# Four attention layers on a graph: where the rows of the node ranges and the first block's one-hot rows are made and loaded

## The chip, the cores and the metric

One core of a Trainium2 chip runs the kernel. The metric is the time of one execution on the device, in microseconds (us); the profile's span runs from the first to the last instruction of the profiled execution.

## The reference, cut to what matters

The model has 3125 nodes with 48 features and 100,000 edges (`src`, `dst`, sorted by `dst`). It runs four small graph networks one after the other. The change touches the first of them, a block of four attention layers (`L = 4`, `H = 48`, `RBF = 40`):

```python
for i in range(L):
    Q = _ln(h @ Wq[i], gq[i], bq[i])
    K = _ln(h @ Wk[i], gk[i], bk[i])
    qi = Q[src]
    kj = K[dst]
    score = (qi * kj).sum(-1) + 0.1 * (edge_attr * qi[:, :RBF]).sum(-1) + logm[dst]
    smax = jax.ops.segment_max(score, src, num_segments=N)
    es = jnp.exp(jnp.minimum(score - smax[src], 20.0))
    denom = jax.ops.segment_sum(es, src, num_segments=N)
    alpha = es / (denom[src] + 1e-10)
    m = h[dst] @ Wm[i]
    aggi = jax.ops.segment_sum(alpha[:, None] * m, src, num_segments=N)
    z = jnp.concatenate([h, aggi], axis=-1) @ Wu[i]
    z = jnp.where(z > 0, z, 0.01 * z)
    h = _ln(h + z, go[i], bo[i])
```

## The kernel before, in words

**Nodes and edges.** The nodes stand in 25 blocks of 128 (`NB = 25`, `P = 128`). The edges were sorted earlier into 25 blocks by `src`, and within each block into 38 tiles (`KT`) of 128 edges. 37 of these tiles (`NW`) belong to node ranges of `dst`: range `k` is the 128 nodes from `WIN[k]` on. The first 24 ranges (`FINE`) overlap and start at `round(1536 * (k / 24) ** 2)`; the other 13 are the node blocks 12 to 24 themselves. The 38th tile holds edges that fit in no range.

**A layer** is one turn of a hardware loop (`nc.Fori(0, LAYERS)` in `first_part`) over four stages: `node_rows`, `attend`, `cold_softmax`, `node_update`. A stage is a block with one instruction stream for each engine; it ends when all five engines have reached its end, and a barrier of all engines follows (`stage`, line 86 in the profile's rows).

**`node_rows`** makes the rows of all nodes. It goes through five chunks `i` of five node blocks (`CS`): ScalarE and VectorE normalise the products, then split each row into three bf16 parts: ScalarE the upper two (`upper`), VectorE the last (`parts`). The parts of the keys and values go to the SBUF tile `tabp`, those of the queries to `queryp`. SyncE (SP) waits for a chunk's parts and writes `table` (line 908) and `queries` (line 909) to HBM. TensorE makes one last small product at the stage's end (line 955) and waits for ScalarE's copy `wmT` for it.

**`attend`** works on units `u`, four (`q` = 0 to 3, the tile ranges `TAKE[q]`) for each edge block `i`. For a unit, `keys` lets TensorE pick the rows of the edges' ends by one-hot products (line 1578 from the SBUF tile `near`, which holds the rows of the 37 ranges; line 1580 from `queryp`); ScalarE copies (1672); GpSimd (POOL) adds the edge attributes (1536, `add_attr`); VectorE multiplies and sums (1709, 1712). `keys` of unit `u` waits for ScalarE's copy of unit `u - 1` and for VectorE's product of unit `u - 2`:

```python
if u:
    pe.wait_ge(s_rowk, u)
if u >= 2:
    pe.wait_ge(s_dot, u - 1)
```

`add_attr` of the first unit of a block also waits for that block's load of `attr`. SP issues all loads, in the order of its program: ten rows of ranges (`rows_of_nodes(0)`, line 1492), the two one-hot tiles of block 0 (`first(0)`, lines 1498 and 1499), the other 27 ranges, and then `attributes(0)` (line 1504) and what the next blocks need. TensorE starts the stage with `READY = 36` products of 512 columns whose result nobody reads (line 1637).

Of the kernel before, what the change touches and what calls it, by code (L numbers as in the profile page):

```python
# [18 lines left out]
P = 128  # L19
# [9 lines left out]
FINE = 24  # L29
# [831 lines left out]

def node_rows(nc, c, ps, a, layer, h, logm, vec, wqk, wm, wmT, wub, wu, queryp, table, queries, acc, nmax, m):

# [8 lines left out]
    needs = [(s.stop - 1) // 4 + 1 for s in CS]  # L872
    W = H1 + KH
    hT = m.sb("nr_hT", [H, NP])
    qk = m.sb("nr_qk", [P, NB, 2, H])
# [13 lines left out]
    with stage(nc, "node_rows", "w", "vec", "wu", "link", "centred", "scaled", "cols", "turned", "hT", "qk", "got", "sq", "var",  # L889
               "std", "both", "rest", "parts", "upper", "wm", "wmT", "wmu", "wu2", "out") as (  # L890
            block, s_w, s_vec, s_wu, s_link, s_centred, s_scaled, s_cols, s_turned, s_hT, s_qk, s_got, s_sq, s_var, s_std,
            s_both, s_rest, s_parts, s_upper, s_wm, s_wmT, s_wmu, s_wu2, s_out):
        @block.sync
        def _(sp):
            sp.dma_start(wqk[:, 0:H], at(a["Wq"])).then_inc(s_w, 16)
            sp.dma_start(wqk[:, H:2 * H], at(a["Wk"])).then_inc(s_w, 16)
            for n, v in enumerate(["gq", "bq", "gk", "bk"]):
                sp.dma_start(vec[:, n, :], row(a[v])).then_inc(s_vec, 16)
            sp.dma_start(wm[:], at(a["Wm"])).then_inc(s_wu, 16)
            sp.dma_start(wub[:], a["Wu"][bass.ds(layer, 1), H:2 * H, :].rearrange("o k f -> (o k) f")).then_inc(s_wu, 16)  # L900
            sp.dma_start(wu[0:H, :], a["Wu"][bass.ds(layer, 1), 0:H, :].rearrange("o k f -> (o k) f")).then_inc(s_wu, 16)
            for n, v in enumerate(["go", "bo"]):
                sp.dma_start(vec[:, 4 + n, :], row(a[v])).then_inc(s_wu, 16)
            for i, s in enumerate(CS):
                rows = lambda t: t.rearrange("(b p) w -> p b w", p=P)[:, s, :]
                sp.wait_ge(s_parts, 2 * (i + 1))
                sp.wait_ge(s_upper, 4 * (i + 1))
# [3 lines left out]
            sp.wait_ge(s_out, 32 * NC)  # L911

# [10 lines left out]
        def _(pe):  # L923
# [30 lines left out]
            pe.wait_ge(s_wmT, 1)  # L954
            pe.matmul(ps[64:64 + H, 6, 0:H], wmT[:], wub[:], start=True, stop=True).then_inc(s_wmu, 1)

        @block.scalar
        def _(act):
# [17 lines left out]
            def upper(i):  # L976
                s, x, r = CS[i], high(both[:, CS[i], :]), high(rest[:, i % 2])
                act.wait_ge(s_both, i + 1)
                act.copy(queryp[:, s, 0, :], x[:, :, 0:H1]).then_inc(s_upper, 1)
                act.copy(tabp[:, s, 0, :], x[:, :, H1:W]).then_inc(s_upper, 1)  # L980
                act.wait_ge(s_rest, i + 1)
                act.copy(queryp[:, s, 1, :], r[:, :, 0:H1]).then_inc(s_upper, 1)
                act.copy(tabp[:, s, 1, :], r[:, :, H1:W]).then_inc(s_upper, 1)
            done = 0
# [17 lines left out]
        def _(dve):  # L1002
# [440 lines left out]

def attend(nc, c, ps, m, lists, table, near, queryp, dead, sel, off, acc, nmax, spill_dst):

# [13 lines left out]
    VB = 4  # L1459
    READY = 36  # L1460
# [3 lines left out]
    hotT_s, hotT_d = m.sb("at_hotT_s", [P, 4, KT, P], F8), m.sb("at_hotT_d", [P, 4, NW, P], F8)  # L1464
    key = m.sb("at_key", [P, 2, 10, H1])
# [11 lines left out]
    rings = [f"attr{k}" for k in range(2)] + [f"hots{k}" for k in range(2)] + [f"hotT{k}" for k in range(4)] + [  # L1477
        f"far{k}" for k in range(4)] + [f"near{k}" for k in range(Q)]
    turned_bank = ps[:, 7, 128:192].bitcast(BF16)
    with stage(nc, "attend", *names, *rings) as (  # L1480
            block, s_keys, s_rowk, s_key, s_dot, s_score, s_split, s_turned, s_rows, s_laid, s_top, s_max, s_mgot, s_shift,
            s_prob, s_h, s_val, s_rest, s_split2, s_sum, s_added, s_link, *dmas):
        s_attr, s_hots, s_hotT, s_far, s_near = dmas[0:2], dmas[2:4], dmas[4:8], dmas[8:12], dmas[12:]

        @block.sync
        def _(sp):
            flat = lambda v, k: v[:, k].rearrange("p k e -> p (k e)")

# [68 lines left out]
        def _(pe):  # L1557
# [5 lines left out]
            def keys(i, q):  # L1563
                u = Q * i + q
                if q == 0:
                    pe.wait_ge(s_hotT[i % 4], 32 * (i // 4 + 1))
# [58 lines left out]
            def total(i, q):  # L1625
# [846 lines left out]
def first_part(nc, c, m, ps, a, x, h, tmp, table0, embs, embp, mult, logm, list1, lists, spill_dst, starts, mask, trips, base, w1,  # L2472
# [45 lines left out]
    with nc.Fori(0, LAYERS) as layer:  # L2518
        with ExitStack() as ctx0:
            node_rows(nc, c, ps, a, layer, h, logm[:], vec, wqk, wm, wmT, wub, wu, queryp, table, queries, acc[:], nmax[:],  # L2520
                      Memory(nc, ctx0))
        with ExitStack() as ctx0:
            t = Memory(nc, ctx0)
            near = t.sb("near", [P, NW, 3, KH], BF16)
            attend(nc, c, ps, t, lists, table, near, queryp, dead, sel, off, acc, nmax, spill_dst)
        with ExitStack() as ctx0:
# [1066 lines left out]
```

## Time and profile before

| | us |
|---|---|
| median of three runs | 5786.9 |
| lowest and highest run | 5772.91 and 5797.48 |
| the profiled execution's own time | 5777.92 |
| its span, first to last instruction | 5776.3 |
| mean granted TensorE clock in it (1.0 is 2.4 GHz) | 0.816 |

All stages come one after the other on one core, so each microsecond that a stage boundary moves is one of the total, unless a later stage waits for something else. The first layer's `node_rows` starts at 1914 us of the span and its `attend` at 1956 us; the other three layers repeat the pattern. The rows of the next but one section are from the first layer where no more is said.

### The profile page before, as it was taken

The page shows a single profiled execution, that of the slowest core. Times are in us where ns is not written, and L with a number is a line of the kernel's source. Part 1 is how long each engine was busy: PE and PEld are TensorE (multiplying, and loading weights), DVE is VectorE, ACT ScalarE, POOL GpSimd, SP SyncE. Part 2 cuts the span into 40 slices and gives each one's busy share as a digit, 9 for nine tenths or more (in the row PEclk, how much of TensorE's full clock was granted, in tenths as well). Part 3 has the DMA queues.
Part 4 walks back from the last instruction along what each step waited for, and adds up shares of the span by engine and source line. Part 5 has one row for each costly group of instructions (what it writes and reads, how often), then busy time and mean ns, then how long its engine had stood idle before and what let it go on. Part 6 is the DMA issues. An engine that isn't in the chain of part 4 may idle for free. (4 is left out here: it accounts for less than half of the span.)

```text
span 5776.3 us, 186815 instructions
## 1 busy us (share of the span) xinstructions
PE 4309.7 (75%) x79576; PEld 3592.7 (62%) x79576; DVE 3791.9 (66%) x7925; ACT 2250.1 (39%) x7746; POOL 2681.4 (46%) x2702
## 2 busy tenths in 40 slices
PE   7999994046666499759976997599757845877887
PEld 4555552035555388748874887488735733877786
DVE  6888875079998588657765785687576446545244
ACT  3333331046666255435543554355401424101310
POOL 2777777756666177517751775277520510000000
PEclk7666665569998699869987998799877977988897
DMA  9322223167775344234423442344255434000000
GB/s 352 74 73 74 70 68 74 42 150 197 195 201 166 113 161 165 92 109 167 154 92 120 157 154 92 123 154 165 80 88 196 158 106 134 2 9 4 4 4 10
DMA packets 488184, 656.80 MB, mean 114 GB/s; under 512 B 316480, under 2 KB 370372, under 8 KB 484117
## 3 DMA queue, kind: packets, MB, share of 16 engines
q1 hardware_dynamic: 450965, 595.00, 32.7%
q0 software_dynamic: 33856, 48.44, 3.4%
q8 instruction: 645, 10.57, 0.7%
q14 instruction: 222, 1.82, 0.1%
q10 hardware_dynamic: 2496, 0.98, 0.1%
HBM read 464.16 MB, written 180.09 MB: 112 GB/s over the span
## 5 line engine op out<-in xcount | busy, mean ns | idle before, releaser
L299 POOL DMA_INDIRECT edges<-sb_bk_rec,sb_bk_pos x782 | 784.8, 1004 | 323.7 <-issue 234.0
L1688 ACT ACTIVATE sb_at_val<-banks,sb_at_prob 128x49 f32<-128x49 f32 x3800 | 776.0, 326 | 189.7 <-PE banks L1622 183.3
L1727 DVE TENSOR_REDUCE sb_at_tops<-banks 128x1 f32<-128x512 f32 x1000 | 652.5, 661 | 279.1 <-PE banks L1602 276.7
L1578 PE MATMUL banks<-sb_near,sb_at_hotT_d 128*128 128x49 bf16 x11100 | 610.3, 184 | 74.0 <-DVE sb_at_key L1709 44.5
L1536 POOL TENSOR_TENSOR sb_at_key<-sb_at_key,sb_at_attr 128x400 f32<-128x400 f32 (+1 forms) x400 | 371.8, 930 | 581.1 <-ACT sb_at_key L1672 489.9
L1580 PE MATMUL banks<-sb_queryp,sb_at_hotT_s 128*128 128x49 bf16 x11400 | 624.5, 185 | 12.8 <-issue 12.3
L1578 PEld LDWEIGHTS banks<-sb_near,sb_at_hotT_d 128*128 128x128 fp8e4 x11100 | 560.3, 96 | 79.1 <-issue 69.3
L1580 PEld LDWEIGHTS banks<-sb_queryp,sb_at_hotT_s 128*128 128x128 fp8e4 x11400 | 559.5, 96 | 15.7 <-issue 15.7
L1543 POOL TENSOR_TENSOR sb_at_val<-sb_at_val 128x490 f32<-128x490 f32 (+1 forms) x400 | 387.4, 968 | 68.9 <-ACT sb_at_val L1688 67.4
L1672 ACT COPY sb_at_key<-banks 128x490 f32<-128x490 f32 (+1 forms) x400 | 225.3, 563 | 462.9 <-PE banks L1580 460.6
L1545 POOL TENSOR_TENSOR sb_at_val<-sb_at_val 128x490 f32<-128x490 f32 (+1 forms) x400 | 386.6, 966 | 31.4
L1622 PE MATMUL banks<-sb_near,sb_at_hotT_d 128*128 128x49 bf16 x11100 | 358.5, 186 | 34.3 <-ACT sb_at_val L1688 22.6
L1602 PE MATMUL banks<-sb_at_rows,sb_sel 114*128 114x128 bf16 x3800 | 379.0, 220 | 1.2 <-issue 1.2
L1599 PE MATMUL banks<-sb_at_hotT_s,sb_off 128*128 128x512 fp8e4 x1000 | 369.4, 369 | 7.3 <-issue 4.5
L1602 PEld LDWEIGHTS banks<-sb_at_rows,sb_sel 114*128 114x128 bf16 x3800 | 297.0, 97 | 116.1 <-issue 9.2
L1622 PEld LDWEIGHTS banks<-sb_near,sb_at_hotT_d 128*128 128x128 fp8e4 x11100 | 331.7, 97 | 43.1 <-ACT sb_at_val L1688 29.1
L1633 PE MATMUL banks<-sb_at_val,sb_at_hot_s 128*128 128x147 bf16 x3800 | 342.3, 237 | 11.9 <-issue 9.1
L1709 DVE TENSOR_TENSOR sb_at_key<-banks,sb_at_key 128x490 f32<-128x490 f32 (+1 forms) x400 | 253.1, 633 | 143.5 <-POOL sb_at_key L1536 143.5
L1262 POOL TENSOR_TENSOR sb_gt_msg<-sb_gt_msg 128x245 f32<-128x245 f32 (+1 forms) x175 | 239.8, 1370 | 189.9 <-DVE sb_gt_msg L1409 189.2
L1633 PEld LDWEIGHTS banks<-sb_at_val,sb_at_hot_s 128*128 128x128 fp8e4 x3800 | 281.1, 101 | 14.4 <-issue 10.7
L2902 PE MATMUL banks<-sb_conv_parts,sb_C 128*128 128x144 bf16 x3750 | 249.3, 232 | 30.8 <-DVE sb_conv_parts L2852 30.8
L2902 PEld LDWEIGHTS banks<-sb_conv_parts,sb_C 128*128 128x128 bf16 x3750 | 247.6, 101 | 31.9 <-DVE sb_conv_parts L2852 31.9
(692 smaller groups left out, 10166.0 us busy)
## 6 DMA issues: line engine op xcount, KB each, us to landing
sb_at_attr<-attr SPq DMA_DIRECT2D x100, 760.0 KB, 7.5
sb_at_hotT_s<-rows_src_t SPq DMA_DIRECT2D x100, 608.0 KB, 3.9
sb_at_hot_s<-rows_src SPq DMA_DIRECT2D x100, 608.0 KB, 8.6
sb_at_hotT_d<-rows_dst_t SPq DMA_DIRECT2D x100, 592.0 KB, 5.9
edges<-sb_pad SPq DMA_DIRECT2D x95, 460.0 KB, 7.0
sb_gt_rec<-edges SPq DMA_DIRECT2D x25, 1748.0 KB
sb_we_hotT<-rows_dst_t SPq DMA_DIRECT2D x52, 592.0 KB, 5.8
attr<-sb_gt_rec SPq DMA_DIRECT2D x25, 760.0 KB, 13.2
```

Source lines behind the costliest of these rows:

```text
L299: pool.indirect_dma_start(list1, bass.IndirectOffsetOnAxis(pos[:, t:t + 1], 0), rec[:, k, j, :], None).then_inc(sent[k], 16)
L1536: pool.tensor_tensor(key[:, u % 2, 0:n, 0:RBF], key[:, u % 2, 0:n, 0:RBF], attr[:, i % 2, a:b, :], ALU.add).then_inc(s_key, 1)
L1543: pool.tensor_tensor(x[:, 0:n, 1, :], x[:, 0:n, 0, :], halves(0), ALU.subtract).then_inc(s_rest, 1)
L1545: pool.tensor_tensor(x[:, 0:n, 2, :], x[:, 0:n, 1, :], halves(1), ALU.subtract).then_inc(s_split2, 1)
L1578: pe.matmul(ps[:, 0, H1 * j:H1 * j + H1], where, what, start=(n == 0), stop=(n == 2))
L1580: ins = pe.matmul(ps[:, 1 + u % 2, H1 * j:H1 * j + H1], hotT_s[:, i % 4, k, :], queryp[:, i, n, :], start=(n == 0), stop=(n == 2))
L1602: ins = pe.matmul(bank[:, P * j:P * j + P], sel[:, k, :], rows[:, i % 2, :], start=False, stop=(k == ks[-1]))
L1622: ins = pe.matmul(ps[:, 5, H1 * j:H1 * j + H1], where, what, start=(n == 0), stop=(n == 2))
L1633: ins = pe.matmul(ps[:, 6, 0:3 * H1], hot_s[:, i % 2, k, :], high(val[:, v % VB, j].rearrange("p n f -> p (n f)")), start=(k == 0), stop=( ...
L1688: ins = act.mul(val[:, v % VB, j, 0, :], ps[:, 5, H1 * j:H1 * j + H1], prob[:, i % 2, k:k + 1])
L1727: dve.tensor_reduce(tops[:, i % 2, g:g + 1], ps[:, 3 + x % 2, 0:P * len(RG[g])], AX, ALU.max).then_inc(s_top, 1)
L2902: return pe.matmul(ps[:, d % AHEAD, 0:3 * H], C[:, s, P * d:P * d + P], rows(s), start=(s == 0), stop=(s == NB - 1))
```

## The change

Four things change in the layers' stages; what is computed stays the same.

1. `near` and the one-hot tiles are allocated outside both stages. VectorE and ScalarE write the parts of node blocks 12 to 24 straight into `near`, where ranges 24 to 36 stand (`homes`); SP writes `table` from there. Only blocks 0 to 11 stay in `tabp`. The chunk of blocks 10 to 14 falls in two pieces.
2. SP loads the 24 overlapping ranges from `table` within `node_rows` (`windows`, line 936), each group behind a wait for the landing of the table chunks that it reads.
3. SP loads the two one-hot tiles of block 0 within `node_rows` (`ahead`, line 920), ahead of the first table chunk.
4. The 36 products of TensorE move from the start of `attend` to the end of `node_rows` (line 996).

`attend` no longer has loads of `near`, nor the wait for them.

```diff
+    LOW = WIN[FINE] // P
+    READY = 36
+    FINE_OF = [[k for k in range(FINE) if all(WIN[k] + P <= P * s.stop for s in CS[i:i + 1]) and
+                (i == 0 or WIN[k] + P > P * CS[i - 1].stop)] for i in range(NC)]
-    tabp = m.sb("nr_tabp", [P, NB, 3, KH], BF16)
+    tabp = m.sb("nr_tabp", [P, LOW, 3, KH], BF16)
+    def homes(s):
+        low, top = range(s.start, min(s.stop, LOW)), range(max(s.start, LOW), s.stop)
+        kept = [(slice(low[0], low[-1] + 1), tabp[:, low[0]:low[-1] + 1])] if low else []
+        return kept + ([(slice(top[0], top[-1] + 1), near[:, FINE + top[0] - LOW:FINE + top[-1] + 1 - LOW])] if top else [])
...
-                sp.dma_start(rows(table), tabp[:, s].rearrange("p b i f -> p b (i f)")).then_inc(s_out, 16)
-                sp.dma_start(rows(queries), queryp[:, s].rearrange("p b i f -> p b (i f)")).then_inc(s_out, 16)
+            for to, src in ahead:
+                sp.dma_start(to, src).then_inc(s_ahead, 16)
+            def write(i):
+                s = CS[i]
+                sp.wait_ge(s_parts, sum(PARTS[:i + 1]))
+                sp.wait_ge(s_upper, sum(UPPER[:i + 1]))
+                for bs, to in homes(s):
+                    sp.dma_start(rows(table, bs), to.rearrange("p b i f -> p b (i f)")).then_inc(s_table[i], 16)
+                sp.dma_start(rows(queries, s), queryp[:, s].rearrange("p b i f -> p b (i f)")).then_inc(s_out, 16)
+            def windows(i):
+                for j in range(i + 1):
+                    sp.wait_ge(s_table[j], 16 * len(homes(CS[j])))
+                for k in FINE_OF[i]:
+                    sp.dma_start(near[:, k].rearrange("p i f -> p (i f)"), table[WIN[k]:WIN[k] + P, :]).then_inc(s_near, 16)
+            write(0)
+            write(1)
+            windows(0)
+            write(2)
+            windows(1)
+            write(3)
+            windows(2)
+            write(4)
             sp.wait_ge(s_wu, 80)
...
             pe.matmul(ps[64:64 + H, 6, 0:H], wmT[:], wub[:], start=True, stop=True).then_inc(s_wmu, 1)
+            for _ in range(READY):
+                pe.matmul(ps[:, 7, :], c["identb"][:], along(c["identb"][:], 4), start=True, stop=True)
...
-                dve.tensor_tensor(tabp[:, s, 2, :], r[:, :, H1:W], high(r)[:, :, H1:W], ALU.subtract).then_inc(s_parts, 1)
+                for bs, to in homes(s):
+                    of = slice(bs.start - s.start, bs.stop - s.start)
+                    dve.tensor_tensor(to[:, :, 2, :], r[:, of, H1:W], high(r)[:, of, H1:W], ALU.subtract).then_inc(s_parts, 1)
...
-            rows_of_nodes(0)
-            first(0)
-            for q in range(1, Q):
-                rows_of_nodes(q)
             attributes(0)
...
-                if i == 0:
-                    pe.wait_ge(s_near[q], 16 * sum(k < NW for k in TAKE[q]))
...
-            for _ in range(READY):
-                pe.matmul(ps[:, 0, :], c["identb"][:], along(c["identb"][:], 4), start=True, stop=True)
```

**SP's order, end of `node_rows` and start of `attend`.** `nr_tabp` is `tabp`, `rows_src_t` and `rows_dst_t` are the one-hot rows in HBM; `x10` counts equal issues. Before:

```order
L908 DMA table<-sb_nr_tabp 128x5x294
L909 DMA queries<-sb_queryp 128x5x147
L83 UNCONDITIONAL_BRANCH
L1485 UNCONDITIONAL_BRANCH
L1492 DMA sb_near<-table 128x294 x10
L1498 DMA sb_at_hotT_s<-rows_src_t 128x4864
L1499 DMA sb_at_hotT_d<-rows_dst_t 128x4736
L1492 DMA sb_near<-table 128x294 x27
L1504 DMA sb_at_attr<-attr 128x1520
```

The same stretch of SP's program in the changed kernel, from the second table chunk to the first load of `attend`:

```order
L928 DMA table<-sb_nr_tabp 128x5x294
L929 DMA queries<-sb_queryp 128x5x147
L936 DMA sb_near<-table 128x294 x14
L928 DMA table<-sb_nr_tabp 128x2x294
L928 DMA table<-sb_near 128x3x294
L929 DMA queries<-sb_queryp 128x5x147
L936 DMA sb_near<-table 128x294 x7
L928 DMA table<-sb_near 128x5x294
L929 DMA queries<-sb_queryp 128x5x147
L936 DMA sb_near<-table 128x294 x3
L928 DMA table<-sb_near 128x5x294
L929 DMA queries<-sb_queryp 128x5x147
```

37 loads of ranges and two of one-hot rows stood between the stage's branch and `attr`; now 24 loads stand between the table chunks of `node_rows`, and `attr` is the first issue of `attend`.

**TensorE's order at the boundary of the two stages.** Before, from the last product of `node_rows` (`sb_wub`, `sb_wmT`) on:

```order
L955 MATMUL banks<-sb_wub,sb_wmT 48x48
L83 UNCONDITIONAL_BRANCH
L1556 UNCONDITIONAL_BRANCH
L1637 MATMUL banks<-sb_ident_bf 128x512 x36
L1578 MATMUL banks<-sb_near,sb_at_hotT_d 128x49 x3
```

In the changed kernel:

```order
L994 MATMUL banks<-sb_wub,sb_wmT 48x48
L996 MATMUL banks<-sb_ident_bf 128x512 x36
L83 UNCONDITIONAL_BRANCH
L1590 UNCONDITIONAL_BRANCH
L1610 MATMUL banks<-sb_near,sb_at_hotT_d 128x49 x3
```

The 36 products moved from behind the branch to ahead of it, so the barrier now waits for them.

## Rows read from the trace of the kernel before

**Rows 1.** Windows: busy us PE, PEld, DVE, ACT, POOL; clock, DMA share, GB/s.

```profile
1936.00:1948.00 12.00, 0.00 (x0) 0.00 (x0) 11.45 (x23) 4.75 (x13) 0.00 (x0) 0.50 0.46 126
1960.00:1972.00 12.00, 9.71 (x149) 5.85 (x147) 0.00 (x0) 0.82 (x2) 0.00 (x0) 0.99 0.86 241
1972.00:1984.00 12.00, 1.14 (x28) 1.17 (x29) 1.91 (x3) 0.32 (x1) 1.89 (x2) 0.58 0.85 274
1984.00:1996.00 12.00, 8.27 (x223) 7.43 (x221) 7.02 (x12) 2.46 (x5) 4.67 (x5) 0.85 0.80 303
2068.00:2080.00 12.00, 12.00 (x357) 11.39 (x355) 10.46 (x24) 7.45 (x33) 8.21 (x10) 1.00 0.25 88
```

**Rows 2.** Timeline of SP, first layer: start, us, issue, count.

```profile
1920.10 0.35 SPq L903 DMA_DIRECT2D sb_vec<-bo  x1
...
1935.88 0.36 SPq L908 DMA_DIRECT2D table<-sb_nr_tabp  x1
1936.28 0.52 SPq L909 DMA_DIRECT2D queries<-sb_queryp  x1
1940.83 0.36 SPq L908 DMA_DIRECT2D table<-sb_nr_tabp  x1
...
1949.97 0.36 SPq L908 DMA_DIRECT2D table<-sb_nr_tabp  x1
1950.38 0.52 SPq L909 DMA_DIRECT2D queries<-sb_queryp  x1
1956.57 4.61 SPq L1492 DMA_DIRECT2D sb_near<-table  x10
...
1962.17 14.05 SPq L1492 DMA_DIRECT2D sb_near<-table  x27
1976.26 0.43 SPq L1504 DMA_DIRECT2D sb_at_attr<-attr  x1
```

**Rows 3.** Timeline of TensorE at the stage boundary, idle time before in brackets.

```profile
1950.00 0.39 PE L955 MATMUL banks<-sb_wub,sb_wmT 48*48 48x48 f32 x2 [15.84 <-ACT sb_wmT L997]
1956.61 9.73 PE L1637 MATMUL banks<-sb_ident_bf 128*128 128x512 bf16 x36 [6.22 <-PEq L86]
```

**Rows 4.** Timelines of ScalarE, GpSimd and VectorE, their first work on unit 0.

```profile
1969.32 0.57 ACT L1672 COPY sb_at_key<-banks 128x490 f32<-128x490 f32 x1 [18.70 <-PE banks L1580]
1981.03 1.89 POOL L1536 TENSOR_TENSOR sb_at_key<-sb_at_key,sb_at_attr 128x400 f32<-128x400 f32 x2 [22.80 <-DMA sb_at_attr<-attr]
1982.04 0.67 DVE L1709 TENSOR_TENSOR sb_at_key<-banks,sb_at_key 128x490 f32<-128x490 f32 x1 [32.10 <-POOL sb_at_key L1536]
```

**Rows 5.** Line 1536, all layers: what ended GpSimd's idle time.

```profile
  DMA sb_at_attr<-attr: 91.2, 4
```

**Rows 6.** Line 1637, all layers: idle before it, and windows of its four runs.

```profile
  PEq L86: 24.0, 4
...
sum 80.00, PE 38.90 PEld 15.53; mean PE 9.72 PEld 3.88
```

**Rows 7.** DMA issues on the page: count, KB each, median us to landing.

```profile
sb_at_hotT_d<-rows_dst_t SPq DMA_DIRECT2D x100, 592.0 KB, 5.9
sb_near<-table SPq DMA_DIRECT2D x148, 73.5 KB, 2.2
table<-sb_nr_tabp SPq DMA_DIRECT2D x20, 367.5 KB, 3.8
queries<-sb_queryp SPq DMA_DIRECT2D x20, 183.8 KB, 4.9
```

**Rows 8.** Line 1492: ns of an issue, min/median/max.

```profile
L1492 SPq DMA_DIRECT2D sb_near<-table x148: 332/432/1667, 1956.6 to 3693.5; - x148
```

**Rows 9.** Line 1504: its DMA's us to landing, min/median/max.

```profile
DMA to landing us min/median/max: 4.1/7.5/8.7
```

**Rows 10.** Lines 1026 and 1027, VectorE: ns of one, min/median/max.

```profile
L1026 DVE TENSOR_TENSOR sb_queryp<-sb_nr_rest x20: 414/416/418, 1929.9 to 3667.1; 128x245 bf16<-128x245 f32 x20
L1027 DVE TENSOR_TENSOR sb_nr_tabp<-sb_nr_rest x20: 659/661/664, 1930.2 to 3667.4; 128x490 bf16<-128x490 f32 x20
```

More of the change, by code:

```diff
@@ L859, in _, with node_rows @@
             sp.wait_ge(landed, 16 * len(pairs))
-def node_rows(nc, c, ps, a, layer, h, logm, vec, wqk, wm, wmT, wub, wu, queryp, table, queries, acc, nmax, m):
+def node_rows(nc, c, ps, a, layer, h, logm, vec, wqk, wm, wmT, wub, wu, queryp, table, queries, acc, nmax, near, ahead, m):
     CS = [slice(b, b + 5) for b in range(0, NB, 5)]
@@ L889, in node_rows @@
     with stage(nc, "node_rows", "w", "vec", "wu", "link", "centred", "scaled", "cols", "turned", "hT", "qk", "got", "sq", "var",
-               "std", "both", "rest", "parts", "upper", "wm", "wmT", "wmu", "wu2", "out") as (
+               "std", "both", "rest", "parts", "upper", "wm", "wmT", "wmu", "wu2", "out", "near", "ahead",
+               *[f"table{i}" for i in range(NC)]) as (
             block, s_w, s_vec, s_wu, s_link, s_centred, s_scaled, s_cols, s_turned, s_hT, s_qk, s_got, s_sq, s_var, s_std,
-            s_both, s_rest, s_parts, s_upper, s_wm, s_wmT, s_wmu, s_wu2, s_out):
+            s_both, s_rest, s_parts, s_upper, s_wm, s_wmT, s_wmu, s_wu2, s_out, s_near, s_ahead, *s_table):
         @block.sync
@@ L903, in _ @@
                 sp.dma_start(vec[:, 4 + n, :], row(a[v])).then_inc(s_wu, 16)
[L904 to L907, printed above, removed]
[L908 to L911 removed]
+            for to, src in ahead:
+                sp.dma_start(to, src).then_inc(s_ahead, 16)
+            def write(i):
+                s = CS[i]
+                rows = lambda t, bs: t.rearrange("(b p) w -> p b w", p=P)[:, bs, :]
+                sp.wait_ge(s_parts, sum(PARTS[:i + 1]))
[16 more added lines that the diff above has]
+            write(4)
+            sp.wait_ge(s_wu, 80)
+            sp.wait_ge(s_ahead, 16 * len(ahead))
+            sp.wait_ge(s_near, 16 * FINE)
+            sp.wait_ge(s_table[3], 16 * len(homes(CS[3])))
+            sp.wait_ge(s_table[4], 16 * len(homes(CS[4])))
+            sp.wait_ge(s_out, 16 * NC)
         @block.gpsimd
@@ L979, in upper @@
                 act.copy(queryp[:, s, 0, :], x[:, :, 0:H1]).then_inc(s_upper, 1)
-                act.copy(tabp[:, s, 0, :], x[:, :, H1:W]).then_inc(s_upper, 1)
+                for bs, to in homes(s):
+                    act.copy(to[:, :, 0, :], high(both[:, bs, :])[:, :, H1:W]).then_inc(s_upper, 1)
                 act.wait_ge(s_rest, i + 1)
                 act.copy(queryp[:, s, 1, :], r[:, :, 0:H1]).then_inc(s_upper, 1)
-                act.copy(tabp[:, s, 1, :], r[:, :, H1:W]).then_inc(s_upper, 1)
+                for bs, to in homes(s):
+                    act.copy(to[:, :, 1, :], r[:, bs.start - s.start:bs.stop - s.start, H1:W]).then_inc(s_upper, 1)
             done = 0
@@ L1441, with attend @@
 K1, KH = H1, 2 * H1
-def attend(nc, c, ps, m, lists, table, near, queryp, dead, sel, off, acc, nmax, spill_dst):
+def attend(nc, c, ps, m, lists, table, near, hotT_s, hotT_d, queryp, dead, sel, off, acc, nmax, spill_dst):
     TAKE = [range(0, 10), range(10, 20), range(20, 29), range(29, KT)]
@@ L1477, in attend @@
     rings = [f"attr{k}" for k in range(2)] + [f"hots{k}" for k in range(2)] + [f"hotT{k}" for k in range(4)] + [
-        f"far{k}" for k in range(4)] + [f"near{k}" for k in range(Q)]
+        f"far{k}" for k in range(4)]
     turned_bank = ps[:, 7, 128:192].bitcast(BF16)
@@ L1564, in keys @@
                 u = Q * i + q
[L1565 to L1568 removed]
+                if q == 0 and i:
+                    pe.wait_ge(s_hotT[i % 4], 32 * ((i - 1) // 4 + 1 if i % 4 else i // 4))
                 if u:
@@ L2519, in first_part @@
         with ExitStack() as ctx0:
-            node_rows(nc, c, ps, a, layer, h, logm[:], vec, wqk, wm, wmT, wub, wu, queryp, table, queries, acc[:], nmax[:],
-                      Memory(nc, ctx0))
-        with ExitStack() as ctx0:
             t = Memory(nc, ctx0)
             near = t.sb("near", [P, NW, 3, KH], BF16)
-            attend(nc, c, ps, t, lists, table, near, queryp, dead, sel, off, acc, nmax, spill_dst)
+            hotT_s, hotT_d = t.sb("at_hotT_s", [P, 4, KT, P], F8), t.sb("at_hotT_d", [P, 4, NW, P], F8)
+            first = [(hotT_s[:, 0].rearrange("p k e -> p (k e)"), lists["hotT_s"][0]),
+                     (hotT_d[:, 0].rearrange("p k e -> p (k e)"), lists["hotT_d"][0])]
+            with ExitStack() as ctx1:
+                node_rows(nc, c, ps, a, layer, h, logm[:], vec, wqk, wm, wmT, wub, wu, queryp, table, queries, acc[:], nmax[:],
+                          near, first, Memory(nc, ctx1))
+            attend(nc, c, ps, t, lists, table, near, hotT_s, hotT_d, queryp, dead, sel, off, acc, nmax, spill_dst)
         with ExitStack() as ctx0:
```

15 lines of the change are left out of this document (7 added, 8 removed).

## The prediction, made before the changed kernel ran

> **What bounds the kernel now.** I read three views, in this order. First the windows of the first layer [rows 1]. In the middle of `attend` TensorE is busy for all of a 12 us window (2068 to 2080) at the full clock, so that part is bound by TensorE and its length is fixed work. Ahead of it there is a hole: from 1936 to 1948 TensorE does nothing, and from 1972 to 1984 it has 1.14 us of work and VectorE 1.91. Nobody computes there, yet the DMA share is 0.85. The second view, the timelines, says what the hole waits for. SP starts `attend` at 1956.57 and reaches the issue of `attr` only at 1976.26 [rows 2], because 39 issues stand ahead of it: 27 of them take 14.05 us, 0.52 us each. GpSimd's first addition starts at 1981.03, after an idle time that the arrival of `attr` ended, and VectorE's first product starts at 1982.04 after 32.10 us of idling [rows 4]. `keys` of unit 2 needs that product, so TensorE can do units 0 and 1 and then stands still. The third view is the line of the addition over all layers: four waits for `attr`, 91.2 us together [rows 5], 22.8 each, the same as the 22.80 of the first layer. So the pattern repeats, and the interval from SP's first issue to the first addition is 1981.03 - 1956.57 = 24.46 us in each layer. The end of the chain is therefore: SP's queue, `attr`, GpSimd, VectorE, TensorE; neither the warming products nor the one-hot tiles end last.
>
> **What the change does to that chain.** `attr` becomes SP's first issue in `attend`. From its issue to the addition the first layer shows 1981.03 - 1976.26 = 4.77 us [rows 2, 4]; I take 4.8. In the changed kernel the addition also needs TensorE's 60 products of unit 0 and ScalarE's copy. TensorE can begin at once; in the full window it makes 357 products in 12 us [rows 1], so 60 take at most 2.0, and the copy takes 0.57 [rows 4]: 2.6 us, behind which `attr` still ends last. So the interval shrinks from 24.46 to 4.8, by 19.7 us a layer.
> A load of `attr` in the midst of `attend` lands 7.5 us (median) after its issue, 4.1 at least and 8.7 at most [rows 9]. The bounds are therefore 0.7 us better and 3.9 worse a layer; I stay at 4.8, because the load's company is the same as in the first blocks now: the same next issues follow it.
> The Trainium skill (DMA: Bandwidth & Descriptors, Anatomy of one DMA) puts a transfer at about 2.0 us and its bytes at 436 GB/s, an estimate of 3.8 us for this one. With it the gain would be 1.0 us a layer larger, 62 in place of the 58 below; the row, with a load's real company, decides.
>
> **What it does to the start of `attend`.** This is what it costs. Before, `node_rows` ends with the landing of the last `queries`: issued at 1950.38, median 4.9 us to landing [rows 7], so 1955.3, and SP starts at 1956.57: 1.3 us for the barrier. TensorE's last product ends at 1950.39 [rows 3]. From there to the first product of `attend` it idles 24.0 us in four layers, 6.0 each [rows 6]. Now the 36 products come first. They take 9.72 us on the mean of the four layers [rows 6], half clock at the beginning included, since the clock is at 0.50 when they start; before them TensorE idles 15.84 us in both kernels [rows 3], so I keep the 9.72. Then the barrier, 1.3 us. `attend` starts 9.72 + 1.3 - 6.0 = 5.0 us later.
> VectorE's chunk of blocks 10 to 14 makes its last part in two pieces. From 245 elements in 416 ns and 490 in 661 [rows 10] an element costs 1.0 ns and an instruction 171 ns, so one more instruction is 0.17 us, on the chain of VectorE, which is 11.45 of 12 us busy there [rows 1] and sets when TensorE's last product can start. ScalarE's two more copies lie in its idle time (4.75 of 12 busy).
>
> **What hides the moved loads.** SP's program in `node_rows` now has 24 loads of ranges between the table chunks. I lay them out with the 0.52 us of a crowded issue. `windows(0)` begins when the second chunk is issued, 1936.8, and takes 14 x 0.52 = 7.3, to 1944.1. The third chunk was ready at 1940.83 and is late by 3.3 us; its three issues end at 1945.5. `windows(1)`: 7 x 0.52, to 1949.1. The fourth chunk (ready one chunk time, 4.95 us, after 1940.83) to 1950.1, `windows(2)` to 1951.6, the last chunk (ready at 1949.97) to 1952.6. Its `queries` land about 1957. TensorE's products end at 1950.4 + 9.7 = 1960.1. So SP's lateness is covered by them with 3.1 us to spare; without them it would cost 2 us. The waits for table landings cost nothing: the third chunk is issued by 1945 and lands 3.8 us later [rows 7], before `windows(2)` is reached. In bytes: four chunks of 367.5 + 183.8 KB and 24 x 73.5 KB are 4.06 MB; at the 241 GB/s of the window of 1960 to 1972 [rows 1] they need 16.9 us, and from 1935.9 to 1957 there are 21. The two one-hot tiles are issued at 1920.9 and take about 6 us [rows 7]; the first table chunk comes one chunk (4.95 us) ahead of 1935.88, at about 1931, so they are out of its way. What is queued behind the loads on SP is only the table and the queries, and nobody in `node_rows` waits for those.
>
> **Sum.** A layer: 19.7 - 5.0 - 0.17 = 14.5 us. Four layers: 58 us. The profiled execution, 5777.9 us, would take 5720. The median of the runs is 9 us above the profiled one, 5786.9, and gives 5729; I forecast 5728.
>
> **Rivals.**
> 1. *The clock holds, a larger gain.* TensorE's pause ahead of unit 2 was about 11 us (1.14 busy of 12). Now VectorE's product of unit 0 is there at 4.8 + 1.0 + 0.7 = 6.5 us [rows 4], and units 0 and 1 are done at 2.0 + 0.6 + 2.0 = 4.6: 2 us of pause. Now the clock is low for much of the restart: 0.58 in the window of 1972 to 1984 and 0.85 in the next [rows 1], where 0.15 x 12 / 0.5 = 3.6 us are at 1.2 GHz, and about one more in the window ahead. If the clock stays at 2.4 GHz over the short pause, at most half of 5 us, 2.5 a layer, is gained on top: 68 us in all, 5719. Against it: a pause of 1.3 us at the barrier and one of 2 us still stand within 10 us.
> 2. *The clock falls in the barrier's pause, a smaller gain.* The warming products now end ahead of a barrier. If `keys` of units 0 and 1 run at 1.2 GHz, they take up to 4.0 us each, not 2.0. Unit 1's copy then ends 9.2 us after the start (4.0 + 0.6 + 4.0 + 0.6), 2.7 later than the 6.5 of VectorE's product. That is at most 2.7 a layer, gain 47, 5740. If the 36 products themselves never get the high clock that they now have for about 6 of their 9.7 us, they cost 6 more a layer: gain 34, 5753. The Trainium skill (TensorE: Matmul & The Clock Gate, Part 1 and HAM oscillation) says that the clock follows how busy TensorE has been of late, and that waits for data put it back to half rate. By that rule the first form of this rival can be had and the second cannot. The trace agrees so far: 0.50 to 0.58 where TensorE idles, 1.00 where it is full [rows 1].
> 3. *The issues jam, and it is slower.* An issue of such a load took up to 1.667 us [rows 8]. If the 24 loads, now between writes to the same table, all take that, SP is 24 x 1.15 = 27.5 us late, 3.1 of it covered: 24.4 a layer lost against 14.5 won, 40 us slower, 5827. It begins to cost above 0.65 us an issue (3.1 / 24 more than 0.52) and turns the sign at 0.52 + 17.6 / 24 = 1.25. Against it: the median issue is 0.43, and in the hole of rows 1, at 241 to 274 GB/s, 27 in a row kept to 0.52.
> 4. *Nothing is won.* The start of `attend` moves, but a later stretch waits for something that does not, such as loads that lag. Against it: in the middle TensorE is full and the DMA share is 0.25. It would leave 5787.
>
> **How the numbers follow.** Forecast, with `attr` landing between 4.1 and 8.7 us and the barrier 0.3 us to either side of 1.3: 0.68, of which rival 2's first form is a part of 0.25. Rival 1: 0.10. Smaller gains (late `attr` in all layers, 42; rival 2's second form, 34): 0.14. Rival 3: 0.04, rival 4: 0.04. The range reaches from rival 1 with the scatter of the runs (-14 to +11 us around the median) on its low side, 5709, to the case of late `attr` (5787 - 42 = 5745) with 5 more for scatter, 5750. A measurement of this kernel tells differences of about 0.5%, 29 us, from none. All cases but rivals 3 and 4 and a part of the smallest gains are above that: faster 0.90, same 0.06, slower 0.04.
>
> **What the changed profile would show.** Right: SP's first issue of `attend` is `attr`, the first addition follows in about 5 us and not 24; the idle time ahead of TensorE's first product of `attend` is 1.3 us; TensorE's last product of `node_rows` is the 36th warming one; `attend` starts at about 47 us after `node_rows`, was 42. Wrong: SP still issuing table chunks when TensorE is done (rival 3); the addition's wait for `attr` over 8 us; the warming products over 12 us (rival 2); the middle of `attend` no longer full (rival 4). My prediction is wrong if either the barrier is more than 3 us behind TensorE's last product or SP's lateness passes the cover.

## The result, and the profile after

The changed kernel takes 5715.6 us (median of four runs, 5714.19 to 5717.01); the kernel before, run beside it, takes 5782.3 (four runs, 5772.91 to 5797.48). The ratio is 0.9882, with a 95% interval from 0.9859 to 0.9905: 66.6 us faster. The profiled execution's span went from 5776.3 to 5714.5 us, 61.8 less. Forecast were 5728 us and a gain of 58.

SP's timeline of the changed kernel, first layer (start, us, issue, count). In this trace the first issue of `node_rows` is at 1917.31, in that of before at 1914.80.

```profile
1917.31 0.36 SPq L910 DMA_DIRECT2D sb_wqk<-Wq  x1
...
1938.79 0.53 SPq L929 DMA_DIRECT2D queries<-sb_queryp  x1
1939.37 7.14 SPq L936 DMA_DIRECT2D sb_near<-table  x14
1946.61 0.38 SPq L928 DMA_DIRECT2D table<-sb_nr_tabp  x1
...
1948.16 3.44 SPq L936 DMA_DIRECT2D sb_near<-table  x7
1951.70 0.38 SPq L928 DMA_DIRECT2D table<-sb_near  x1
1952.12 0.53 SPq L929 DMA_DIRECT2D queries<-sb_queryp  x1
1952.75 2.34 SPq L936 DMA_DIRECT2D sb_near<-table  x3
1955.19 0.38 SPq L928 DMA_DIRECT2D table<-sb_near  x1
1955.61 0.53 SPq L929 DMA_DIRECT2D queries<-sb_queryp  x1
1963.50 0.33 SPq L1542 DMA_DIRECT2D sb_at_attr<-attr  x1
```

The 24 loads of ranges take 12.9 us, 0.54 each, and SP issues without a pause from 1939.37 on. `attr` is the first issue of `attend`, where before 39 others stood ahead of it [rows 2]. The timelines of TensorE, GpSimd and VectorE at the same place (idle time ahead in brackets, with what ended it):

```profile
1952.59 0.39 PE L994 MATMUL banks<-sb_wub,sb_wmT 48*48 48x48 f32 x2 [15.93 <-ACT sb_wmT L1040]
1952.91 9.72 PE L996 MATMUL banks<-sb_ident_bf 128*128 128x512 bf16 x36
1963.54 0.23 PE L1610 MATMUL banks<-sb_near,sb_at_hotT_d 128*128 128x49 bf16 x3 [0.91 <-PEq L86]
...
1969.83 0.23 PE L1610 MATMUL banks<-sb_near,sb_at_hotT_d 128*128 128x49 bf16 x3 [2.27 <-DVE sb_at_key L1739]
...
1968.01 1.88 POOL L1570 TENSOR_TENSOR sb_at_key<-sb_at_key,sb_at_attr 128x400 f32<-128x400 f32 x2 [2.85 <-DMA sb_at_attr<-attr]
...
1969.01 0.67 DVE L1739 TENSOR_TENSOR sb_at_key<-banks,sb_at_key 128x490 f32<-128x490 f32 x1 [16.48 <-POOL sb_at_key L1570]
```

From SP's first issue of `attend` to the first addition it is now 1968.01 - 1963.50 = 4.5 us, before 24.46. The products of unit 0 start 0.91 us after the last warming product, and VectorE idles 16.48 us ahead of its first product, not 32.10 [rows 4]. Unit 2 starts at 1969.83, after a wait of 2.27 us for VectorE. What ended GpSimd's idle time ahead of line 1570, all layers, against the 91.2 us of [rows 5]:

```profile
  DMA sb_at_attr<-attr: 11.0, 4
```

The windows, which answer to [rows 1] (the same columns); those around the stage boundary first:

```profile
1944.00:1956.00 12.00, 3.41 (x10) 1.40 (x11) 8.19 (x15) 4.12 (x11) 0.00 (x0) 0.50 0.96 204
1950.00:1952.00 2.00, 0.00 (x0) 0.00 (x0) 1.93 (x4) 1.37 (x4) 0.00 (x0) 0.50 1.01 138
1956.00:1958.00 2.00, 2.00 (x10) 0.83 (x9) 0.00 (x0) 0.00 (x0) 0.00 (x0) 0.86 1.07 250
...
1960.00:1970.00 10.00, 6.17 (x140) 4.36 (x138) 0.95 (x2) 1.14 (x2) 2.87 (x3) 1.00 0.57 180
1970.00:1972.50 2.50, 2.02 (x54) 1.88 (x49) 1.62 (x3) 0.45 (x1) 0.00 (x0) 0.54 0.91 344
...
1972.00:1984.00 12.00, 8.66 (x206) 7.40 (x206) 6.79 (x12) 2.45 (x5) 4.67 (x5) 0.79 0.82 315
1984.00:1996.00 12.00, 10.05 (x294) 8.78 (x290) 11.47 (x25) 3.19 (x6) 4.39 (x5) 1.00 0.36 126
...
2068.00:2080.00 12.00, 11.52 (x347) 10.82 (x345) 9.60 (x23) 6.68 (x30) 9.13 (x11) 1.00 0.26 102
```

The hole is gone: from 1972 to 1984 TensorE works 8.66 us of 12, before 1.14. Two readings were not in the forecast. The DMA engines are nearly always busy from 1944 to 1956 (0.96), at 204 GB/s, and in one stretch of 2 us at only 138. And the clock is 1.00 during units 0 and 1 and through the short wait ahead of unit 2 (1960 to 1970), but falls to 0.54 just behind it, in the first products of unit 2 (1970 to 1972.5).

**Where the 61.8 us of span came from.** Counted from the first issue of `node_rows`, the first addition came after 66.24, 66.07, 68.52 and 65.95 us in the four layers, sum 266.8. Now it comes after 50.70, 53.45, 51.55 and 51.34, sum 207.0. That is 59.7 us (from unrounded times), 14.9 a layer. From the first addition to the next layer took 504.85, 505.70 and 506.81 us and takes 502.35, 504.49 and 505.00: 5.5 us less in three layers. The layers start 2.5 us later, and behind the last layer's first addition 1.0 is lost. 59.7 + 5.5 - 2.5 - 1.0 = 61.7. Only the first term is explained by the change; the others are of the size in which such stretches scatter from run to run (last section).

### The profile page after: what moved, and what is told of

The parts are those of the page before. It is cut to its first block and busy times, and to the rows that moved or that the text cites. A ratio compares the mean times of both kernels' runs of the same rounds, so it can differ in the third digit from the quotient of the medians.

```text
span 5714.5 us, 186702 instructions
## 1 busy us (share of the span) xinstructions
PE 4266.2 (75%) x79491; PEld 3587.6 (63%) x79576; DVE 3792.0 (66%) x7929; ACT 2244.4 (39%) x7754; POOL 2676.4 (47%) x2702
## 5 line engine op out<-in xcount | busy, mean ns | idle before, releaser
L1610 PE MATMUL banks<-sb_near,sb_at_hotT_d 128*128 128x49 bf16 x11100 | 609.8, 184 | 36.4 <-issue 18.6
L1612 PE MATMUL banks<-sb_queryp,sb_at_hotT_s 128*128 128x49 bf16 x11400 | 624.3, 185 | 14.1 <-issue 13.9
L1654 PE MATMUL banks<-sb_near,sb_at_hotT_d 128*128 128x49 bf16 x11100 | 358.8, 186 | 35.7 <-ACT sb_at_val L1718 22.6
```

The source lines that it names most:

```text
L1610: pe.matmul(ps[:, 0, H1 * j:H1 * j + H1], where, what, start=(n == 0), stop=(n == 2))
L1612: ins = pe.matmul(ps[:, 1 + u % 2, H1 * j:H1 * j + H1], hotT_s[:, i % 4, k, :], queryp[:, i, n, :], start=(n == 0), stop=(n == 2))
L1654: ins = pe.matmul(ps[:, 5, H1 * j:H1 * j + H1], where, what, start=(n == 0), stop=(n == 2))
```

## The experiments

Every kernel was timed against the kernel before, run beside it. The first four share one set, in which it took 5780.9 us. The second and the third set of four ran on other chips, where it took 6011.9 and 6011.6 us; some 190 us of the difference lie ahead of the layers, there the ratios and the times within a layer are what can be compared. In the third set the changed kernel itself ran once more (c1); the second has no such run, so e5 to e8 are held against c1, which ran on another chip.

All times below are means over the four layers of the profiled run, in us. "Last product" is the end of TensorE's last product of `node_rows` that is not a warming one, counted from the first issue of the stage. "To `attend`" is from there to SP's first issue in `attend`, then from there to the first addition, and from the first to the fifth addition.

| kernel | ratio, 95% interval | last product | to `attend` | to 1st addition | 1st to 5th |
|---|---|---|---|---|---|
| before (profile as shown) | 1 | 36.3 | 6.0 | 24.5 | 10.3 |
| changed | 0.9882 [0.9859, 0.9905] | 36.3 | 11.0 | 4.4 | 10.1 |
| e1_warm_in_attend | 0.9938 [0.9922, 0.9955] | 37.4 | 10.3 | 12.1 | 9.1 |
| e2_no_warm | 0.9912 [0.9896, 0.9929] | 36.7 | 10.2 | 4.5 | 11.4 |
| e3_attr_first | 0.9968 [0.9956, 0.998] | 37.6 | 6.1 | 13.9 | 17.3 |
| e4_hot_in_attend | 0.9939 [0.9918, 0.996] | 37.0 | 10.8 | 9.2 | 9.3 |
| second set: e5_ranges_in_attend | 0.9966 [0.9954, 0.9977] | 36.4 | 10.9 | 10.8 | 14.0 |
| e6_warm_in_idle | 0.9896 [0.9879, 0.9914] | 37.6 | 11.2 | 4.5 | 11.3 |
| e7_fillers | 0.9912 [0.9895, 0.9929] | 37.0 | 11.3 | 4.5 | 9.7 |
| e8_loads_last | 0.9907 [0.9893, 0.9921] | 38.0 | 11.7 | 4.5 | 10.2 |
| third set: c1_changed_again | 0.9907 [0.9891, 0.9924] | 35.7 | 11.4 | 4.5 | 10.7 |
| c2_no_warm_again | 0.9921 [0.9902, 0.9939] | 38.3 | 11.3 | 4.4 | 11.5 |
| c3_warm_in_idle_again | 0.9897 [0.988, 0.9913] | 37.6 | 11.3 | 4.5 | 9.7 |
| c4_double_warm | 0.9968 [0.9956, 0.998] | 37.1 | 18.7 | 5.6 | 10.9 |

### The parts of the change that shorten the queue

**e3_attr_first**: the kernel before, `attributes(0)` put first.

```diff
+            attributes(0)
             rows_of_nodes(0)
             first(0)
             for q in range(1, Q):
                 rows_of_nodes(q)
-            attributes(0)
```

> The kernel before with one line moved: SP issues attr ahead of the ranges and the one-hot tiles, all else as before. Queue theory: the first addition comes at about 13.5 us after the start of attend instead of 24.5, but units 2 and 3 then wait for ranges 20 to 36, which land at about 18 and 22 us, and block 1 for its one-hot tiles; 5.5 to 8 us a layer are won: 5750 to 5760 against 5782. Rival (only loading in node_rows helps, or attr is not what ends last): within 5 us of the kernel before.

Measured: 5762.2 us, 18.7 less than before and 2 above the upper end that was expected. SP's first issue of `attend`, GpSimd's first additions, and TensorE ahead of two of its next units, in the timeline of the first layer:

```profile
1960.48 0.34 SPq L1504 DMA_DIRECT2D sb_at_attr<-attr  x1
...
1974.22 0.98 POOL L1536 TENSOR_TENSOR sb_at_key<-sb_at_key,sb_at_attr 128x400 f32<-128x400 f32 x1 [12.08 <-ACT sb_at_key L1672]
1977.55 0.95 POOL L1536 TENSOR_TENSOR sb_at_key<-sb_at_key,sb_at_attr 128x400 f32<-128x400 f32 x1 [2.36 <-ACT sb_at_key L1672]
...
1978.31 0.30 PE L1578 MATMUL banks<-sb_near,sb_at_hotT_d 128*128 128x49 bf16 x3 [1.44 <-DMA sb_near<-table]
1982.03 0.31 PE L1578 MATMUL banks<-sb_near,sb_at_hotT_d 128*128 128x49 bf16 x3 [1.29 <-DMA sb_near<-table]
```

The addition no longer waits for `attr` but for ScalarE's copy, so the warming products and the products of unit 0 are next in line; behind those TensorE waits for the loads of the ranges. The interval to the first addition is 10.6 us shorter, and the next four units take 7.0 longer. So `attr`'s place in the queue was the wait that ended last, and right behind it stood the ranges: one cheap move gets less than a third of what the whole change gets.

**e4_hot_in_attend**: the changed kernel, with the two one-hot tiles of block 0 loaded first in `attend`.

```diff
-                          near, first, Memory(nc, ctx1))
+                          near, [], Memory(nc, ctx1))
...
+            first(0)
             attributes(0)
...
-                if q == 0 and i:
+                if q == 0:
```

> The changed kernel with the one-hot tiles of block 0 loaded at the start of attend, ahead of attr. Queue theory: both tiles land about 6.5 us after the start, the first addition at about 8.8 instead of 4.4: +4.4 us a layer, 5733. Rival (they were hidden behind something else, or crowded node_rows): within 4 us of the changed kernel.

Measured: 5740.9 us (five runs: three from 5737 to 5741, two at 5762; the profile is of one of the latter). SP's first issues of `attend` and the first addition:

```profile
1968.30 0.33 SPq L1535 DMA_DIRECT2D sb_at_hotT_s<-rows_src_t  x1
1968.68 0.43 SPq L1536 DMA_DIRECT2D sb_at_hotT_d<-rows_dst_t  x1
1969.15 0.42 SPq L1541 DMA_DIRECT2D sb_at_attr<-attr  x1
...
1977.35 0.98 POOL L1570 TENSOR_TENSOR sb_at_key<-sb_at_key,sb_at_attr 128x400 f32<-128x400 f32 x1 [7.40 <-DMA sb_at_attr<-attr]
```

`attr` is issued 0.85 us after the stage's start, and the addition that waits for it begins 9.05 us after that start, in the changed kernel 4.51, since 1.2 MB are under way ahead of it. On the mean it is 4.8 us a layer, somewhat more than expected: what an issue ahead of `attr` costs is its bytes, not its 0.4 us on the queue.

**e5_ranges_in_attend**: the changed kernel, with the 24 ranges loaded in `attend` behind `attributes(0)`, each group of tiles with a wait of its own.

```diff
-            windows(0)
             write(2)
-            windows(1)
             write(3)
-            windows(2)
             write(4)
...
             attributes(0)
+            for q in range(Q):
+                for k in TAKE[q]:
+                    if k < FINE:
+                        sp.dma_start(near[:, k].rearrange("p i f -> p (i f)"), table[WIN[k]:WIN[k] + P, :]).then_inc(s_near[q], 16)
```

> The changed kernel with the 24 loads of overlapping ranges back in attend, right behind attr; blocks 12 to 24 still go straight into near. Queue theory: unit 0 waits for its ten ranges (landing 7.8 us after the start), unit 1 for 20 (13 us), and block 1's one-hot tiles are issued 12.5 us later: 8 to 10 us a layer are lost, 5748 to 5756. Rival (the ranges made in place carry the gain, the loads' place does not matter): within 8 us of the changed kernel's 5716.

Measured: 23.7 us less than before, where the changed kernel (c1) wins 57.5 against the same time of before: more than half of the gain is lost, 6.4 us a layer to the first addition and 3.2 up to the fifth. The loss in all is 33.8 us against c1, within the 32 to 40 that had been expected. The ranges are needed first by unit 0, and 24 issues take 12.9 us in `attend` as well.

### The place of the warming products

**e1_warm_in_attend**: the 36 products back at the start of `attend`.

```diff
-            for _ in range(READY):
-                pe.matmul(ps[:, 7, :], c["identb"][:], along(c["identb"][:], 4), start=True, stop=True)
...
+            for _ in range(36):
+                pe.matmul(ps[:, 0, :], c["identb"][:], along(c["identb"][:], 4), start=True, stop=True)
```

> The changed kernel with one part undone: the 36 warming products stand at the start of attend again. Queue theory (the gain is that attr no longer waits behind SP's other issues): node_rows ends with SP's last queries, about 44.5 us after its start instead of 46.2, but then 9.7 us of products, unit 0's 60 products (1.7) and the copy (0.6) come ahead of the first addition, which is 5.8 us a layer later than in the changed kernel: +23 us, 5739. Rival (it does not matter where the products stand, attr ends last either way): 5709 to 5716.

Measured: 5745.8 us. TensorE's and GpSimd's timelines:

```profile
1960.39 9.93 PE L1667 MATMUL banks<-sb_ident_bf 128*128 128x512 bf16 x36 [10.24 <-PEq L86]
...
1972.59 0.98 POOL L1568 TENSOR_TENSOR sb_at_key<-sb_at_key,sb_at_attr 128x400 f32<-128x400 f32 x1 [10.58 <-ACT sb_at_key L1702]
```

With `attr` landed early the products are on the path: counted from the last product, the first addition comes 7.0 us a layer later than in the changed kernel (22.4 against 15.4; 5.8 had been expected). And the stage hardly ends earlier without them, 10.24 us after the last product instead of the 10.63 (9.72 + 0.91) above.

**e2_no_warm** and **c2_no_warm_again**: the products taken out.

```diff
-            for _ in range(READY):
-                pe.matmul(ps[:, 7, :], c["identb"][:], along(c["identb"][:], 4), start=True, stop=True)
```

> The changed kernel without the 36 warming products (they compute nothing that is used). Queue theory: attend starts when SP's last queries have landed, 1.7 us a layer earlier, and attr lands 4.4 us after that; units 0 and 1 at 1.2 GHz still hide behind attr: -7 us, 5709. Rival (the products carry a part of the gain, since the clock of the first units is what the start hangs on): 2 us or more a layer slower, 5724 or more.

> No warming products at all, a second time. Theory (the products at the end of node_rows are nearly free, since SP's last landings end the stage almost as late, and they speed up the fill by about 1.4 us a layer): attend starts 0.4 to 1.1 us earlier a layer, the fill up to the fifth addition is about 1.4 us longer, so within 5 us of the changed kernel, on the slower side. Rival (the products do earn something beyond the fill, as the first run of this variant seemed to say): 10 us slower than the changed kernel or more.

Measured: 5726.7 us in the first set, 11 slower than the changed kernel, where a gain had been forecast, but with ratios whose intervals overlap. In the third set it is 1.4 us slower by the medians and about 8 by the ratios (0.9921 and 0.9907), again with overlapping intervals. SP and TensorE in the first layer of c2_no_warm_again:

```profile
2138.11 0.53 SPq L929 DMA_DIRECT2D queries<-sb_queryp  x1
2146.80 0.33 SPq L1540 DMA_DIRECT2D sb_at_attr<-attr  x1
...
2135.01 0.39 PE L994 MATMUL banks<-sb_wub,sb_wmT 48*48 48x48 f32 x2 [15.93 <-ACT sb_wmT L1038]
2146.83 0.29 PE L1608 MATMUL banks<-sb_near,sb_at_hotT_d 128*128 128x49 bf16 x3 [11.43 <-PEq L86]
```

TensorE has nothing to do and yet waits 11.43 us for the barrier; `attend` follows 8.7 us after SP's last issue. So SP's last landings, not TensorE, end the stage. Three products of unit 0 take 0.29 us, where they took 0.23 behind the warming products, and the first five additions take 0.8 to 1.4 us longer. Together with the slightly earlier start of `attend` that comes to 0.6 us a layer, some 2.5 us in all. Whether the products earn more than that these runs do not settle.

**e6_warm_in_idle** and **c3_warm_in_idle_again**: the products ahead of TensorE's wait for `wmT`, in its idle time.

```diff
+            for _ in range(READY):
+                pe.matmul(ps[:, 7, :], c["identb"][:], along(c["identb"][:], 4), start=True, stop=True)
             pe.wait_ge(s_wmT, 1)
```

> The changed kernel with the 36 products ahead of the wait for ScalarE's copy wmT, where TensorE idles 16 us anyway: they end about 6 us before the last product of node_rows. Theory after the run without them (units of the first blocks at 1.2 GHz cost 2 us a layer, and SP's last landing, not TensorE, then ends node_rows): the clock has fallen again by the start of attend, and the time is that of the kernel without the products, 5720 to 5730. Rival (having warmed up at some time is enough): 5708 to 5713, since the stage also ends 0.8 us earlier.

> The 36 products ahead of the wait for wmT, where TensorE idles. Theory (SP's landings set the start of attend, so hiding the products wins nothing): within 5 us of the changed kernel. Rival (TensorE's products set the start, and hiding them pays): 5 to 15 us faster than the changed kernel.

TensorE's timeline in the first layer of c3_warm_in_idle_again:

```profile
2123.91 10.62 PE L994 MATMUL banks<-sb_ident_bf 128*128 128x512 bf16 x36
2139.90 0.39 PE L996 MATMUL banks<-sb_wub,sb_wmT 48*48 48x48 f32 x2 [5.38 <-ACT sb_wmT L1040]
2151.45 0.28 PE L1610 MATMUL banks<-sb_near,sb_at_hotT_d 128*128 128x49 bf16 x3 [11.15 <-PEq L86]
```

In c3 the products are hidden, and still TensorE waits 11.15 us for the barrier, as long as without them. The clock has fallen again by then, as the theory for e6 said: three products of unit 0 take 0.28 us, as without the warming ones. Measured: ratios 0.9896 and 0.9897, the lowest of their sets. Against c1_changed_again c3 is 7.6 us faster, more than the 5 that the first theory allowed, but the intervals overlap and the profiles show nothing for it: `attend` starts no earlier. It may be a slightly better version; these runs don't settle it. The two runs also show how little the last column of the table carries to the total: it is one kernel, the first five additions take 11.3 us in e6 and 9.7 in c3, and the ratios are the same.

**c4_double_warm**: `READY = 72`.

> 72 warming products in place of 36 at the end of node_rows. Theory (the 36 just fill the cover of SP's landings, anything more is added to the path): each further product is 0.216 us at the full clock, 36 of them 7.8 us, so attend starts 7.8 us later a layer, 31 us in all, 0.994 of the kernel before. Rival (they are still covered): same as the changed kernel.

Measured: 0.9968, 35 us slower than c1_changed_again. To `attend` it is 7.3 us a layer more (expected 7.8), and the first addition comes another 1.2 later, its wait for `attr` being longer. Why `attr` takes longer behind an idle queue was not looked into. Beyond 36, then, nearly all of the added work is on the path.

**c1_changed_again**: the changed kernel itself.

> The changed kernel itself, beside three variants of it, so that they can be compared under the same conditions. Both theories: 0.988 to 0.990 of the kernel before.

Measured: 57.5 us less than before.

### The order of SP's last issues, and the clock in the short wait

**e8_loads_last**: `write(4)` ahead of `windows(2)`, and `READY = 28`.

```diff
-            windows(2)
             write(4)
+            windows(2)
```

> The changed kernel with the last table chunk issued ahead of the last three range loads, and 28 warming products instead of 36. Theory (SP issues without a pause from the second chunk to the end and its last queries land 7 us after their issue, so SP and TensorE end node_rows nearly together): the write lands 1.5 to 2 us earlier and TensorE ends 1.7 earlier, so attend starts about 1.5 us a layer earlier, 5709. Rival (landing is set by the crowd of transfers, not by the order): within 2 us of the changed kernel, or slower through a clock that rises later.

Measured: 0.9907, and `attend` starts 11.7 us after the last product, no earlier than with the order of the changed kernel (11.4 in c1). What SP waits for at the stage's end has changed with the order: now the three range loads (24.1 us in the four layers), in the changed kernel the table chunk and the last `queries` (16.9 and 4.0). So the last writes are issued sooner, but then the loads land last; the time is the same, as the rival said. Eight warming products fewer make no difference to that, since TensorE waits 2.7 to 4.2 us for the barrier here.

**e7_fillers**: ten products more in TensorE's wait ahead of unit 2, to hold the clock.

```diff
+                if u == 2:
+                    for _ in range(10):
+                        pe.matmul(ps[:, 3, :], c["identb"][:], along(c["identb"][:], 4), start=True, stop=True)
```

> The changed kernel with ten more unused products of 512 columns (2.1 us at full clock) between keys of units 1 and 2, where TensorE pauses 2.3 us. Theory (this pause lets the clock fall to 1.2 GHz for units 2 to 4): the granted clock stays at 2.4 GHz through the first block and 1 to 2 us a layer are won: 5708 to 5712. Rival (the clock falls for another reason, or the fillers push unit 2 later): 5716 or up to 5724.

Measured: 0.9912, which is nearer to the rival's forecast. The clock is held (1.00 in the row below, where the changed kernel had 0.54 at this place), and the first five additions take 9.7 us (9.46 to 9.90; c1: 10.44 to 11.43). That is 1.0 us a layer less than in c1, but no more than the scatter of this column: two layers of the changed kernel took 9.62 and 9.63 without fillers. No gain is seen in the total; from the first to the hundredth addition a layer takes 417.6 us, in c1 415.8. The window of that wait in the first layer:

```profile
2165.00:2170.00 5.00, 4.38 (x96) 2.94 (x92) 2.57 (x4) 1.10 (x2) 2.38 (x3) 1.00 0.99 336
```

## Why the prediction was right, and where its steps were off

**The chain.** Right. SP's queue, `attr`, GpSimd, VectorE was what ended last: e3, which moves only `attr`, shortens the interval by 10.6 us, and e4 and e5, which put other loads back, lengthen it by 4.8 and 6.4.

**The interval to the first addition.** Forecast 4.8 us, measured 4.51, 4.32, 4.44 and 4.38. The Trainium skill's estimate in the prediction (DMA: Bandwidth & Descriptors, Anatomy of one DMA) was 1.0 us below the row; the measurement lies between the two. The page gives its figures for loads that GpSimd issues, and this one is issued by SP, so it is no test of the page.

**The start of `attend`.** Forecast 5.0 us later, measured 47.35 - 42.22 = 5.1. Two of its terms were off in opposite directions: the barrier took 0.9 us behind TensorE's last product, not 1.3, and the 36 products 10.22 on the mean, not 9.72. The 0.17 us laid out for VectorE's extra instruction is hardly to be seen: leaving out the one layer of each kernel that lost time at its start (last section), the last product comes at 35.6 to 35.8 us, before at 35.6 to 35.7. The products' own windows in the four layers (PE busy, PEld busy, clock, DMA share, GB/s):

```profile
1951.00:1965.00 14.00, 9.72 (x36) 3.90 (x36) 0.80 0.67 132
2507.00:2521.00 14.00, 10.11 (x36) 4.00 (x36) 0.79 0.69 129
3062.00:3076.00 14.00, 10.55 (x36) 4.11 (x36) 0.74 0.68 126
3619.00:3633.00 14.00, 10.52 (x36) 4.11 (x36) 0.76 0.68 125
```

**The cover for the moved loads.** This is the step that was mis-sized. "SP's lateness is covered by them with 3.1 us to spare" was right in its sign alone. In the first layer SP's last issue ended 3.2 us after TensorE's last product (1956.14 against 1952.98), where 2.2 had been laid out, and the `queries` landed 5.4 us after that, where 4.4 had been. From issue to landing that is 5.9 us, and 6.4, 6.7 and 6.2 in the other layers; the prediction had 4.9. The products ended at 1962.63 and the landing came at about 1961.5: 1.1 us to spare, on the mean of the layers 1.5. A second count gives less: in e1 and e2, without products in that place, `attend` starts 10.25 us after the last product, in the changed kernel 11.03, so the products add only 0.8. On the chip of the third set nothing is to spare: 11.4 us with the products and 11.3 without.

"Without them it would cost 2 us" was too low as well: against the 5.96 us of the kernel before, the 10.25 of e1 and e2 are 4.3 us more. So moving the products cost less than 1 us a layer, not 5, and the moved loads and writes cost the rest. The start of `attend` came out as forecast because the two stand side by side and end together; that the cover sufficed is in part luck. A likely reason for the late landing is the term for the bytes. At the 241 GB/s that the prediction took, the 4.06 MB need 16.9 us; at the 204 of 1944 to 1956, with the engines busy for 0.96 of the time, 19.9. No run separates this from other reasons.

**The clock.** Rival 2's first form did not come: in the first layer units 0 and 1 ran at 1.00 after the pause of 0.91 us. Rival 1 did not come either: behind the wait of 2.27 us ahead of unit 2 the clock fell to 0.54, and the first five additions take 10.1 us, before 10.3. The Trainium skill (TensorE: Matmul & The Clock Gate, HAM oscillation) has waits for data put the clock back to half rate; the trace agrees for the wait ahead of unit 2. e7 holds the clock there, and nothing is seen of it in the total.

**The other rivals.** Rival 3 is refuted: 24 issues between the writes took 0.54 us each. Rival 4 as well: from the first to the hundredth addition a layer took 415.9 us and takes 414.9.

**The sum.** The gain up to the first additions is 59.7 us, forecast 58; the total is 66.6 in the medians and 57.5 in the repetition c1. Two slips in the range changed nothing: rival 1's 5719 less the scatter of 14 is 5705, not 5709, and the second form of rival 2 (5753) lay outside it.

## What to carry to other kernels

When an engine idles at the start of a stage, read which issue on the load queue it waits for, and count what stands ahead of it, issues and bytes; then look at what stands right behind it, since moving the one load alone (e3) gave less than a third of what moving all gave. Loads moved into an earlier stage are paid at that stage's end: lay out their landings with some reserve, since behind a crowd of transfers the last one took 5.9 to 6.7 us and not the usual 4.9. Work that only warms TensorE belongs where another engine ends the stage, and just so much of it as that lateness covers: 36 products cost under 1 us a layer there, 36 more cost 8.5, and the same 36 behind the barrier made the first addition 7.0 us later.

## What the runs showed of the hardware

- From 1944 to 1956, with range loads (128 rows of 588 bytes, 73.5 KB) and the writes of `table` and `queries` under way together, the 16 DMA engines were busy for 0.96 of the time and moved 204 GB/s; in 1970 to 1972.5 the large loads of `attend` moved 344 GB/s at a share of 0.91.
- In e8 the last table chunk was issued ahead of three loads instead of behind them, and the stage ended no sooner.
- In layers 2 to 4 TensorE starts `node_rows` 3 to 4.7 us late in every kernel, with the idle time put down to "issue". Whether that matters goes with the clock: where the window below shows 0.71 the lateness is made good (last product at 35.6 to 36.2 us), where it stays at 0.50 it is not (38.0 us and more). Both occur within one execution of one kernel; the changed kernel's layers 2 and 3:

```profile
2472.00:2488.00 16.00, 13.98 (x59) 10.67 (x60) 6.07 (x14) 6.97 (x15) 2.86 (x6) 0.50 0.51 92
3030.00:3046.00 16.00, 10.77 (x69) 8.44 (x70) 8.68 (x20) 9.73 (x21) 2.86 (x6) 0.71 0.34 102
```

In the 14 profiles this befell between none and three of the layers, 1.2 to 4.2 us each, so up to some 10 us of a total (c2) can come from it, whatever the kernel. The later bodies scatter too (414.9 to 417.9 us a layer between first and hundredth addition in the kernels whose ranges are loaded early). So does the part ahead of the layers, which is the same in all kernels: the first layer starts at 1912 to 1922 us in the first set and the two profiles of the result, and at 2099 to 2114 in the other sets. Together they hide every effect below about 10 us here. What decides the clock there was not tried.
